# A decoder of four layers on one core: the openings of two cross-attentions one group later, their query loads in one piece, bulk inputs and masks one stage later

## What is computed

```python
x = x + L0_attn(layernorm(x))             # softmax(q k^T * scale) v, then a projection
x = x + L0_xattn(layernorm(x), context)   # keys and values from context, 512 of them
x = x + L0_ffn(layernorm(x))              # routed experts
...
x = x + L3_attn(layernorm(x), mask)
x = x + L3_xattn(layernorm(x), context)
x = x + L3_ffn(layernorm(x))

def L0_xattn(x, context):
    q = heads(x @ q_w + q_b); k, v = heads(context @ kv_w + kv_b)
    attn = softmax(where(context_mask, -inf, q @ k.T * scale))
    return (attn @ v) @ proj_w + proj_b
```

## Time and profile before

| | |
|---|---|
| time of three runs | 1519.13, 1526.16, 1527.60 us; median 1526.16 |
| profiled execution | 1519.38 us, its span 1517.2 us |
| mean granted TensorE clock | 0.877 |
| L0_attn, L0_xattn | about 0 to 124 us and 126 to 248 us of the span |
| L3_attn, L3_xattn | about 1232 to 1340 us and 1341 to 1481 us |

### The profile page before, as it was taken

How to read it: one execution, slowest core, us unless ns; L and a number is a source line. 1 busy time by engine, 2 the same in 40 slices (tenths; PEclk the granted TensorE clock), 3 DMA queues, 4 the chain that set the end, 5 groups by cost and what they waited for, 6 DMA issues and landing times. The chain is left out here.

```text
span 1517.2 us, 26546 instructions
## 1 busy us (share of the span) xinstructions
PE 1210.4 (80%) x9465; PEld 749.9 (49%) x9465; DVE 901.1 (59%) x2363; ACT 701.5 (46%) x1344; POOL 273.7 (18%) x549
## 2 busy tenths in 40 slices
PE   4877998686596398467999999999947769869983
PEld 2333334585243288255666666666637723323332
DVE  5656883433677445585776766667741076657756
ACT  3662884121453022122665765666704435626663
POOL 3411110453010255200000000000006404211110
PEclk9786999899798589786999999999978878979995
DMA  7541211584602467100000000000045542211100
GB/s 179 157 115 28 58 36 79 160 277 133 184 2 90 142 211 229 36 1 0 1 1 1 1 1 1 2 1 1 1 133 184 153 137 72 54 38 44 49 7 14
DMA packets 88323, 114.33 MB, mean 75 GB/s; under 512 B 11505, under 2 KB 68542, under 8 KB 87726
## 3 DMA queue, kind: packets, MB, share of 16 engines
q1 hardware_dynamic: 83746, 103.52, 23.1%
q0 software_dynamic: 4448, 9.12, 1.9%
HBM read 85.79 MB, written 25.82 MB: 74 GB/s over the span
## 5 line engine op out<-in xcount | busy, mean ns | idle before, releaser
L862 DVE TENSOR_REDUCE mx<-ps 128x4 f32<-128x1024 f32 (+1 forms) x128 | 154.2, 1222 | 51.5 <-PE ps L786 49.9
L1015 PE MATMUL ps<-probs,vaug 128*32 128x256 f32 (+1 forms) x1792 | 147.8, 405 | 15.4 <-ACT probs L981 9.7
L2494 DVE CUSTOM_DVE_ANT_0 wring<-ps,probs 128x768 f32<-128x768 f32 x128 | 122.6, 958 | 56.9 <-PE ps L2366 56.8
L2450 ACT COPY qs<-ps 128x768 f32<-128x768 f32 x128 | 102.3, 800 | 97.7 <-PE ps L2373 97.7
L971 ACT ACTIVATE probs<-ps 128x1024 f32<-128x1024 f32 x96 | 98.2, 1023 | 80.2 <-PE ps L835 79.9
L976 ACT ACTIVATE probs<-ps 128x512 f32<-128x512 f32 x192 | 106.5, 595 | 49.9 <-PE ps L929 47.9
L243 POOL TENSOR_TENSOR rstd<-veps,mhalf 128x8 f32<-128x8 f32 x12 | 19.9, 1660 | 568.2 <-DVE veps L228 538.7
L2432 ACT ACTIVATE wring<-wring,r 128x768 f32<-128x768 f32 x128 | 120.8, 944 | 2.9 <-DVE r L2497 2.9
L2373 PE MATMUL ps<-ident,wring 128*128 128x128 f32 x768 | 110.4, 281 | 3.2 <-DVE wring L2531 3.2
L786 PE MATMUL ps<-ks,qs 49*128 49x256 bf16 (+1 forms) x512 | 83.5, 369 | 29.5 <-DVE mx L857 15.2
L2373 PEld LDWEIGHTS ps<-ident,wring 128*128 128x128 f32 x768 | 84.5, 141 | 39.4 <-issue 35.3
(11 more groups left out here) (345 smaller groups left out, 2359.8 us busy)
## 6 DMA issues: line engine op xcount, KB each, us to landing
wring<-in_L_ffn_w SPq DMA_DIRECT2D x19, 768.0 KB
wring<-in_L_ffn_w SPq DMA_DIRECT2D x32, 384.0 KB
wring<-in_L_ffn_w SPq DMA_DIRECT2D x19, 514.0 KB
qs<-scr_q SPq DMA_DIRECT2D x18, 192.0 KB
probs<-in_L_ffn_w SPq DMA_DIRECT2D x8, 384.0 KB
probs<-in_L_ffn_w SPq DMA_DIRECT2D x4, 768.0 KB
scr_k<-probs SPq DMA_DIRECT2D x21, 128.0 KB, 2.8
scr_x<-w SPq DMA_DIRECT2D x1, 2496.0 KB
```

The source lines that it names most:

```text
L862: dve.tensor_reduce(out, src, AX.X, ALU.max, negate=True).then_inc(a_max.sem, 1)
L1015: ins = pe.matmul(ps[32 * j:32 * j + 32, self.av_bank(s), q0:S], vaug[:, s % 2, kt, j, :], probs[:, s % 2, j, at:at + S - q0], start=(kt = ...
L2450: act.copy(self.pT[:, g % 2, j, :, k * P:(k + 1) * P], self.buffer("turn", i, 0, KV).rearrange("p (t n) -> p t n", n=P)).then_inc(self.out ...
L2494: dve.tensor_tensor_reduce(self.sc[:, s, :], src, self.maskb[:, u // (2 * PR), :], 1.0, -3.0e38, ALU.add, ALU.max, self.top[:, s:s + 1]).t ...
```

## The change

It makes five edits.

- The turns of h and the query matmuls of a batch's opening come one group later. Batches 0 and 1 stay in the self-attention; batch 2 moves to outputs 0 and 1 of the cross-attention, batch 3 to outputs 2 and 3 (it was 1 and 2). The splits of the queries and their spills move along. The statistics stay, and h of batch 2 stays in the self-attention.
- L0_xattn's values come later: from step 0, unit 2 and 6 to step 0, unit 6 and step 1, unit 2.
- The stacked queries of a batch are loaded by one pair of DMAs of all eight head pairs, with group 4b−2, in the place of a pair of DMAs with each of the groups 4b−4 to 4b−1. They are counted on `stacked[0]` alone.
- The bulk inputs go out three bundles at a time with groups 12 to 15 of L0_xattn. What is wanted earlier (L0_xattn's v and o weights, two bias rows) is loaded at the start: one DMA more, and the weights' one is 256 KB larger.
- `masks_vector` runs on DVE ahead of the last `y` of L0_xattn.

```diff
-    slices = [[8 + 2 * int(i == 0 and c["mask"] == "row") for i in range(4)] for c in ATTN]
+    slices = [[6 + int(i == 0) * (2 + 2 * int(c["mask"] == "row")) for i in range(4)] for c in ATTN]
...
+            if b == 2:
+                pe.wait_ge(v_sb.sem, v_sb.at(self.n, self.nv))
             for t in range(2):
                 ins = pe.transpose(bank(6, S + t * P, S + t * P + P), h[:, 2 * b + t, :], ident[:, :])
...
-        def q_load_sync(self, sp, b, first_pair, end_pair):
-
-            pairs, landed = slice(first_pair, end_pair), stacked[first_pair // 2] if b else first_quad
+        def q_load_sync(self, sp, b):
+
+            landed = stacked[0] if b else first_quad
             sp.wait_ge(spilled[b % 2].sem, spilled[b % 2].at(self.n, b // 2 + 1))
...
-                sp.dma_start(dst[:, pairs, :], src[:, pairs, :]).then_inc(landed.sem, 16)
+                sp.dma_start(dst, src).then_inc(landed.sem, 16)
...
-                steps = {(9, 2): "n_stats", (10, 0): "n_h", (12, 0): "qr", (12, 2): "qp2", (13, 0): "qp3"}
+                steps = {(9, 2): "n_stats", (10, 0): "n_h", (13, 0): "qr", (13, 2): "qp2", (14, 0): "qp3"}
                 for b in range(B):
                     what = steps.get((s - 4 * b, u))
-                    if what and (b < 3 or what == "n_stats"):
+                    if what and (b < 2 or what == "n_stats" or b < 3 and what == "n_h"):
...
-                steps = {(0, 2): [("val", 0), ("val", 1)], (0, 3): [("n_h", 3)], (0, 4): [("v_sb", 1)], (0, 6): [("v_sb", 0), ("val", 2), ("val", 3)],
-                         (1, 0): [("v_sb", 2)], (1, 2): [("v_sb", 3)], (6, 2): [("qr", 3)],
-                         (6, 5): [("qp2", 3)], (7, 2): [("qp3", 3)]}
+                steps = {(0, 3): [("n_h", 3)], (0, 6): [("val", 0), ("val", 1)], (1, 0): [("v_sb", 1)], (1, 2): [("v_sb", 0), ("val", 2), ("val", 3)],
+                         (1, 4): [("v_sb", 2)], (1, 6): [("v_sb", 3)]}
+                for b in (2, 3):
+                    steps |= {(2 * b + 1, 2): [("qr", b)], (2 * b + 1, 5): [("qp2", b)], (2 * b + 2, 2): [("qp3", b)]}
...
-            if self.next and 6 <= o and o % 4 >= 2:
-                yield ("n_tp", "nq")[o % 4 - 2], o // 4 - 1, o
-            elif self.prev and o in (1, 2):
-                yield ("n_tp", "nq")[o - 1], 3, o
+            if self.next and 7 <= o < 13 and o % 4 in (3, 0):
+                yield ("n_tp" if o % 4 else "nq"), (o - 7) // 4, o
+            elif self.prev and o < 4:
+                yield ("n_tp", "nq")[o % 2], 2 + o // 2, o
...
-                if self.n == 0:
+                if self.n == 1:
                     late_inputs(sp, g)
...
-                if self.cross and 6 <= g < 9:
-                    self.q_spill_sync(sp, 3, g - 6)
+                if self.cross and g in (4, 5, 7, 8):
+                    for k in (0,) if g in (4, 7) else (1, 2):
+                        self.q_spill_sync(sp, 2 + int(g > 6), k)
...
-                    self.q_load_sync(sp, g // NQ + 1, g % NQ * 2, g % NQ * 2 + 2)
+                    if g % NQ == 2:
+                        self.q_load_sync(sp, g // NQ + 1)
...
+                    if self.n == 1 and s == B - 1:
+                        masks_vector(dve)
                     self.y_vector(dve, s)
...
-    early = slice(W_OF["L0_xattn_q"] * D, W_OF["L0_xattn_v"] * D)
+    early = slice(W_OF["L0_xattn_q"] * D, W_OF["L0_xattn_o"] * D + D)
...
-        bundles[5] = ((brow[:, 2:9, :], rows[:, 2:9, :]),)
+        bundles[5] = ((brow[:, 4:9, :], rows[:, 4:9, :]),)
...
-        for dst, src in bundles.get(g - 3, ()):
-            sp.dma_start(dst, src).then_inc(loaded, 16)
+        for i in range(3 * (g - 12), 3 * (g - 11)):
+            for dst, src in bundles.get(i, ()):
+                sp.dma_start(dst, src).then_inc(loaded, 16)
```

More of the change, by code:

```diff
@@ L336, in keys_tensor @@
             if self.n == 1:
-                pe.wait_ge(written, 16 * 4)
+                pe.wait_ge(written, 16 * 5)
             pe.wait_ge(proj_f.sem, proj_f.at(self.n - 1, 4))
@@ L498, in ahead_sync @@
             if g == 15:
-                self.q_load_sync(sp, 0, 0, 8)
+                self.q_load_sync(sp, 0)
         def late_sync(self, sp):
-            for b in (1, 2):
-                for k in range(3):
-                    self.q_spill_sync(sp, b, k)
+            for k in range(3):
+                self.q_spill_sync(sp, 1, k)
             sp.wait_ge(b_mm.sem, b_mm.at(self.n - 1, G * units[self.n - 1]))
@@ L525, in ahead_masked_at @@
             if self.next:
-                steps = {17: "n_stats", 18: "n_h", 23: "qr", 24: "qp2", 25: "qp3"}
+                steps = {17: "n_stats", 18: "n_h", 25: "qr", 26: "qp2", 27: "qp3"}
                 for b in range(B):
                     what = steps.get(t - 8 * b)
-                    if what and (b < 3 or what == "n_stats"):
+                    if what and (b < 2 or what == "n_stats" or b < 3 and what == "n_h"):
                         yield what, b, 0
@@ L532, in ahead_masked_at @@
                 steps = {1: [("val", 0), ("val", 1), ("n_h", 3)], 2: [("v_sb", 1)], 3: [("v_sb", 0), ("val", 2), ("val", 3)], 4: [("v_sb", 2)],
-                         5: [("v_sb", 3)], 24: [("qr", 3)], 25: [("qp2", 3)], 26: [("qp3", 3)]}
+                         5: [("v_sb", 3)]}
+                for b in (2, 3):
+                    steps |= {8 * b + 4: [("qr", b)], 8 * b + 5: [("qp2", b)], 8 * b + 6: [("qp3", b)]}
                 for what, b in steps.get(t, ()):
@@ L537, in beside @@
         def beside(self, o):
-            if self.next and 6 <= o and o % 4 >= 2:
-                yield ("n_tp", "nq")[o % 4 - 2], o // 4 - 1, o
-            elif self.prev and o in (1, 2):
-                yield ("n_tp", "nq")[o - 1], 3, o
+            if self.next and 7 <= o < 13 and o % 4 in (3, 0):
+                yield ("n_tp" if o % 4 else "nq"), (o - 7) // 4, o
+            elif self.prev and o < 4:
+                yield ("n_tp", "nq")[o % 2], 2 + o // 2, o
         def evicted(self, o):
[L546 to L549, removed]
+            if self.next and 7 <= o < 13 and o % 4 in (3, 0):
+                yield ("hT" if o % 4 else "qf"), (o - 7) // 4, o
+            elif self.prev and o < 4:
+                yield ("hT", "qf")[o % 2], 2 + o // 2, o
         def value_tensor(self, pe, c):
@@ L1219, in tensor @@
                 elif what == "n_tp":
-                    pe.wait_ge(o_sb.sem, o_sb.at(self.n, u))
+                    if u:
+                        pe.wait_ge(o_sb.sem, o_sb.at(self.n, u))
                     (self.next or self).hT_tensor(pe, s)
@@ L1780, in gpsimd @@
                 pool.wait_ge(placed.sem, placed.at(m, 2))
-                pool.wait_ge(written, 16 * 6)
+                pool.wait_ge(written, 16 * 7)
                 for t in range(NT):
@@ L2770, in _ @@
         for dst, src in ((w[:, early], a["w"][:, early]), (ctxT[:, 0:T], a["ctxT"][:, 0:T]), (ctxT[:, T:], a["ctxT"][:, T:]),
-                         (mrow_raw[:, :], a["mask_row"])):
+                         (mrow_raw[:, :], a["mask_row"]), (brow[:, 2:4, :], rows[:, 2:4, :])):
             sp.dma_start(dst, src).then_inc(written, 16)
@@ L2792, in _ @@
         others[11].out_sync(sp)
-        sp.wait_ge(written, 16 * 10)
+        sp.wait_ge(written, 16 * 11)
     @block.gpsimd
@@ L2805, in _ @@
                 pool.wait_ge(first_in, 16 * 4)
-            if s == 1:
+            if s == 2:
                 pool.wait_ge(loaded, LOADED)
@@ L2813, in _ @@
                     link(pool, pchain, pool.tensor_scalar(bscaled[:, :], bcol[:, :], SCALE, None, ALU.mult))
-                    pool.wait_ge(written, 16 * 4)
+                    pool.wait_ge(written, 16 * 5)
                     pool.tensor_scalar(mrow[:, :], mrow_raw[:, :], -BIG, None, ALU.mult).then_inc(consts, 1)
@@ L2847, in _ @@
                 subs[s].vector(dve)
-                if s == 0:
-                    masks_vector(dve)
                 dve.wait_ge(y_out.sem, y_out.at(subs[s].n, B))
```

## The result

The changed kernel takes 1545.31 us (median of 4 runs, 1540.44 to 1545.37), the kernel before 1523.76 (4 runs, 1519.13 to 1527.60). The ratio is 1.0148, with a 95% interval of 1.0109 to 1.0186: slower by 1.5%, 21.6 us between the medians. Executions in the slower state of the chip (here one of e4 at 1717.88 us and one of the kernel before at 1530.60, on the same chip) are left out of all ratios. The two profiled executions lie further apart, with spans of 1543.1 and 1517.2 us, 25.9. What follows is read from these two.

The account below looks back on a forecast made before the run. It took TensorE in program order to bound the cross-attentions and a chain of waits the seam. Stalls 22.1, clock 9.6 and costs 6.3 less gains 19.1 gave +18.9 us on 1526.16: 1545.1 us, 8-in-10 range 1522 to 1557.

Parts of the forecast that it names:

- The query load: First scores of groups 4, 8 and 12, both cross-attentions: TensorE waits for the late merged load, six times, +22.1 us.
- The landing: Merged query load in the cross-attentions: it lands 1.9 us after the issue's end, read off the falling DMA share.
- The clock: After each of the six cross-attention waits, matmuls run at a lower granted clock: 1.6 us each, +9.6 us.
- Gains of the later openings: L0's self-attention loses its wait for h, −4.3 us; the seams of L0 and L3 lose batch 2's opening, −6.5 and −3.7.
- The seam of L0: Between L0's two attentions: batch 2's opening leaves the drain, −6.5 us, and the mask instructions leave DVE, −2.1 us.
- The relief of SP: L0's cross-attention: fewer SP loads per group remove the 2.03 us `mT` wait and most of its clock loss, −2.5 us.
- Values and third opening: L0's cross-attention: later value matmuls cost 2.5 us, batch 2's opening moved there 1.8 us (0.5 in L3).
- The masks ahead of the last y: End of L0's cross-attention: DVE's wait of 2.22 us covers the masks' 2.1, so cost 0.
- The start: Before the first projection: 256 KB more to load costs 0.5 us, between 0 and 1.
- rival 3: L0's cross-attention, groups 12 to 15: bulk loads delay `mT` loads and masks, 6 us more, 1551 us; chance 0.08.
- Rival 1: Cross-attentions: merged loads land before the scores want them, no stalls, −12.8 us, 1513.4 us; chance 0.13.
- Rival 2: Cross-attentions: stalls cost only 2.0 us each with clock, partly absorbed, −0.8 us, 1525 us; chance 0.17.

Follow-up runs that it names:

- e4: Kernel before with only the bulk inputs, start loads and masks moved: 1517.53 us against 1519.01, ratio 0.9983.
- e1: Changed kernel with the merged query loads issued one group earlier, with group 4b-3: 1503.09 us against 1519.01 for the kernel before, ratio 0.9893.
- e3: Kernel before with only the query loads merged into one pair, issued with group 4b-2: 1561.63 us against 1519.01, ratio 1.0288.
- e2: Changed kernel with the query loads ahead of the six key loads in SP's block: 1529.66 us against 1519.01 for the kernel before, ratio 1.0076.
- e6: e1 with bulk inputs, start loads and masks put back as before: 1493.67 us against 1505.54 for the kernel before, ratio 0.9933.
- e8: e1 with the mask row's loads issued one group later: 1486.66 us against 1505.54 for the kernel before, ratio 0.9888.
- e10: e1 with L0_xattn's values put back, batch 3's mask row moved to group 9 and its queries loaded ahead there: 1504.49 us against 1521.25, ratio 0.9874.
- e9: The kernel of e1 again on another chip: 1501.58 us against 1521.25 for the kernel before, ratio 0.9864.
- e5: Kernel before with only the query loads merged into one pair, issued with group 4b-3: 1499.12 us against 1505.54, ratio 0.9983.
- e7: e1 with L0_xattn's values put back at the steps of before: 1487.56 us against 1505.54 for the kernel before, ratio 0.9891.

## Why the prediction was right, point by point

- **The query load.** The steps were as predicted: SP reached it 4.68 us after the turn (4.69 said), the issue took 0.83 (0.93), TensorE wanted it 3.71 after the turn (3.45). The landing was mis-sized: 3.24 us after the issue's end (3.0 to 3.4 over the six) and not 1.9. It was read off the DMA share, which falls about a microsecond before TensorE starts; the other 0.3 stay open. So the standing is 29.3 us, not 22.1. e1 and e3 show this part alone from both sides, e2 its composition.
- **The clock.** 10.5 us against 9.6, by e1 and the changed kernel.
- **Gains of the later openings.** In L0's self-attention 4.3 was said, and 5.9 came for openings and bulk together. With only one of the two the stretch takes 67.4 or 67.3 us (e4, e6), which is not told from the 66.8 to 70.2 with neither. The text put bulk at a cost of 1.0, and no run shows one: e4 is at 0.9983, and with the openings the move gave some 7 us (e6). The seam of L0 gave 8.1 against 6.5 and 2.1, less the part of 2.5 for the values that lies in it; that of L3 3.2 against 3.7.
- **The relief of SP.** This step failed. The wait for `mT` near group 9 stayed (1.78 us against 2.03 in the earlier trace rows). The wait comes from the block of group 8, which has the mask row, spills and key loads, and which the change did not make short enough (e8, e10). 2.5 us too many in the gains.
- **The costs.** Values and third opening: L0's cross-attention takes 98.45 us in e1 and 99.87 in e9 against 95.41 in e5 and 96.34 before, so 2 to 4 us against 2.5 + 1.8; about 1 of it is the values, where 2.5 was said (e7, e10). In L3 it is 1.1 against 0.5 (116.24 in e1, 115.12 before). The masks ahead of the last y were covered: DVE had them from 254.37 to 256.47 and x followed at 256.50, 2.33 us behind the division's start, where it came after 2.50 before. The start cost nothing that shows, 32.55 us to the first turn against 32.84; the 256 KB more there are 128 KB of weights and 128 KB of bias rows, and not all in the weights' load. Bulk in the way of the turns (rival 3) did not happen: from the turn of group 12 on the groups take 5.74, 5.74 and 5.67 us, as before (5.74, 5.73 and 5.64), after one of 6.70.
- **The sum.** +18.9 was forecast against the median; 21.6 was measured between medians and 25.9 between the profiled executions. The stalls were 7.2 larger and the clock 0.9, the relief of SP did not come (2.5), and the seam and the self-attention gave about 2 to 3 more than said. That 1545.1 meets 1545.31 is luck: these errors cancel only in part, the profiled executions show more than the medians, and the median before, 1526.16 of three runs, fell to 1523.76 with the fourth. Rival 1 is what e1 makes true by moving the load, with 1503.1 us on its chip (15.9 below the kernel before) where −12.8 had been worked out. Rival 2 fails: nothing absorbed a stall.

The Trainium skill's rule to coalesce small transfers ("DMA: Bandwidth & Descriptors", Rules for kernel authors) does not decide here. Merging moved the time by 0.17%, within what can be told from nothing, when it was early (e5), and by 2.9% the other way when it was late (e3).

## What to carry to other kernels

When loads that went out in pieces are merged, the merged load must land by the time of the *first* piece, not of the mean one: take the issuing engine's place in its own order, add the issue and the landing, and compare with the first reader. In a stage that one engine bounds in program order, a wait costs more than its length, since the clock goes with it: six of 4.1 to 5.6 us cost 6.6 each here. And an edit that shows nothing alone (the bulk move, 0.9983) is worth a second try on top of the others: there, taking it back cost some 7 us.

## What the hardware showed that was not expected

- The landing of 384 KB is seen by the waiting engine about 1.0 us after the DMA engines are done (share 0.01 in the window from 143.80, 0.00 from 143.90, matmul at 144.85), and 3.24 us after the issue ended, though the engines were busy for only about 2 us of that. A landing time read off the DMA share is too early by about a microsecond. The 1.9 of the prediction plus 1.0 would have been 2.9.
- The granted clock fell to its lower level (0.50, 1.2 GHz) while TensorE still stood, in the window from 142.00; it had had no work since 139.81. From turn to turn the mean was 0.64: 8.33 us busy for work that took 6.78 in e1 at a mean of 0.82.
